# One operand fewer in the step sizes' product, and the residuals' statistics behind the x products

## What is computed

```python
h = h + attn(layernorm(h))            # a selective state-space block, below
h = h + ffn(layernorm(h))             # 32 experts, each token goes to 8
# inside attn, with x = layernorm(h):
zxbcdt = einsum('btd,pd->btp', x, W_in)            # z, x, B, C, dt
dt = softplus(dt_raw + dt_bias)                    # 16 heads
xBC = silu(conv_b + sum(shifted(xBC, k) * conv_w[:, k] for k in range(4)))
# h_t = h_{t-1} * exp(dt_t * A) + dt_t * B_t x_t ;  y_t = h_t C_t + D x_t
y = y * silu(z)
y = y * rsqrt(mean(y * y) + eps) * norm_w
return einsum('bti,di->btd', y, W_out)
```

## Time and profile before

| what | us |
|---|---|
| median of 3 runs | 1726.41 (1725.41 to 1730.03) |
| the profiled execution | 1733.31 |
| its span, first to last instruction | 1731.6 |
| PE busy in the span | 1558.0 (90%) |
| DVE busy | 969.8 (56%) |
| POOL busy | 788.6 (46%) |
| ACT busy | 728.9 (42%) |

### The profile page before, as it was taken

The page is one execution under the profiler, slowest core; times in us unless marked ns, Lnnn a source line. Parts: engine busy times, 40 slices in busy tenths (PEclk is TensorE's granted clock), DMA queues, the critical chain, the costliest instruction groups (busy, mean ns, idle before and its releaser), DMA issues. The chain is left out here.

```text
span 1731.6 us, 31397 instructions
## 1 busy us (share of the span) xinstructions
PE 1558.0 (90%) x9263; PEld 1133.3 (65%) x9264; DVE 969.8 (56%) x2309; ACT 728.9 (42%) x1592; POOL 788.6 (46%) x678
## 2 busy tenths in 40 slices
PE   7999999987699999999999760499999999999997
PEld 7999999984566685775766430265565666565564
DVE  5555554532678989999999454143343434333343
ACT  2525343431856857858658100133333333333332
POOL 4330300011042247777777577455445555454554
PEclk9999999997889999999999575699999999999999
DMA  7210000003444443543532110477677777767665
GB/s 274 80 62 1 13 1 13 1 19 110 144 118 119 130 138 97 156 132 94 157 89 78 33 39 2 158 166 178 162 164 162 161 188 173 180 156 191 157 112 99
DMA packets 97702, 195.19 MB, mean 113 GB/s; under 512 B 38391, under 2 KB 46879, under 8 KB 92880
## 3 DMA queue, kind: packets, MB, share of 16 engines
q0 software_dynamic: 36992, 88.26, 23.4%
q1 hardware_dynamic: 60624, 105.78, 19.9%
HBM read 144.15 MB, written 49.84 MB: 112 GB/s over the span
## 5 line engine op out<-in xcount | busy, mean ns | idle before, releaser
L1902 PE MATMUL moe_ps_gu<-moe_wgu,moe_xt 128*128 x960 | 333.6, 491 | 0.0
L1760 POOL DMA_INDIRECT out_h<-moe_yy,moe_idx_s x121 | 190.8, 1577 | 260.3 <-DVE moe_idx_s L1822 111.0
L1028 POOL DMA_INDIRECT scratch_slots<-lay_toki,lay_slot x192 | 217.9, 1135 | 57.5 <-issue 57.5
L1902 PEld LDWEIGHTS moe_ps_gu<-moe_wgu,moe_xt 128*128 128x128 f32 x960 | 174.4, 192 | 97.0 <-issue 1.8
L1799 ACT ACTIVATE moe_sl<-moe_ps_gu 128x192 f32<-128x192 f32 x120 | 39.6, 330 | 365.0 <-PE moe_ps_gu L1902 365.0
L1299 PE MATMUL lay_ring<-head_wout,lay_yb 128*128 128x512 f32 x384 | 171.2, 600 | 0.0
L1431 DVE SCALAR_TENSOR_TENSOR lay_xa<-lay_ring,head_cw,lay_xa 128x378 f32<-128x378 f32 (+5 forms) x240 | 141.6, 609 | 51.4 <-ACT lay_xa L1086 45.5
L1215 PE MATMUL lay_ring<-lay_xnt,win_sb 128*128 128x128 f32 (+2 forms) x1152 | 163.3, 288 | 1.5 <-ACT lay_xnt L1118 0.7
L1754 POOL DMA_INDIRECT moe_xg<-scratch_xg,moe_idx_g x123 | 131.1, 1066 | 48.0 <-issue 23.9
L1215 PEld LDWEIGHTS lay_ring<-lay_xnt,win_sb 128*128 128x128 f32 (+2 forms) x1152 | 146.5, 195 | 6.9 <-issue 2.1
L247 POOL TENSOR_TENSOR tok_vv<-tok_w 128x512 f32<-128x512 f32 x16 | 16.6, 1038 | 261.4 <-ACT tok_w L449 227.1
(11 more groups left out here) (291 smaller groups left out, 2944.2 us busy)
## 6 DMA issues: line engine op xcount, KB each, us to landing
lay_m<-scratch_cum SPq DMA_DIRECT2D x16, 1536.0 KB
moe_wgu<-in_wgu SPq DMA_DIRECT2D x32, 768.0 KB, 5.7
moe_wd<-in_wd SPq DMA_DIRECT2D x32, 384.0 KB, 7.7
out_h<-lay_hres SPq DMA_DIRECT2D x48, 128.0 KB
scratch_xg<-lay_x SPq DMA_DIRECT2D x48, 128.0 KB
win_sb<-in_win SPq DMA_DIRECT2D x1, 4384.0 KB, 15.9
tok_u_raw<-in_tok_u SPq DMA_DIRECT2D x16, 256.0 KB, 4.4
tok_v_raw<-in_tok_v SPq DMA_DIRECT2D x16, 256.0 KB, 5.1
```

What stands on the lines that cost most here:

```text
L1028: pool.indirect_dma_start(out=a["slots"], out_offset=bass.IndirectOffsetOnAxis(ap=slot[i % 2][:, j, k:k + 1], axis=0), in_=toki[i % 2][:, ...
L1760: pool.indirect_dma_start(out=a["out"], out_offset=bass.IndirectOffsetOnAxis(ap=idx_s[n][:, 0:1], axis=0), in_=yy[n][:], in_offset=None, b ...
L1902: last = mm(ps_gu[b][:], xt[b][:, t], wgu[:, bass.ds(r * KD + t, 1)].rearrange("p o n -> p (o n)"), start=t == 0, stop=t == KD - 1)
```

## The change

Three things. The step sizes' product multiplied the softplus by A (one value per partition) and by a tile of ones that it read in full; now it multiplies by A alone, with one operand of many elements. The three residuals follow each other, and their statistics with the variances' last step form a new function `residual_stats`, which is called behind the six x products. The shift of the routed rows moves behind the convs of B and C.

```diff
-                    own.step(v.scalar_tensor_tensor(dtr[:], td_in[32:48], ea[:], ones[0:NH].unsqueeze(1).to_broadcast([NH, 2, SEQ]),
-                                                    ALU.mult, ALU.mult))
+
+                    own.step(v.tensor_scalar(dtr[:], td_in[32:48], ea[:], None, ALU.mult))
...
-                    dve.wait_ge(res_done, i * 3 + j + 1)
-                    own.step(v.bn_stats(st[:], h[:, j]))
-                    own.step(v.bn_aggr(mv[:, j], st[:]))
-                    if j == 2:
-                        v.tensor_scalar(ve[:], mv[:, :, 1], EPS, None, ALU.add).then_inc(ve2_done, 1)
+
+                def residual_stats(i):
+                    h = hres[i % 2]
+                    for j in range(N_BLK):
+                        dve.wait_ge(res_done, i * 3 + j + 1)
+                        own.step(v.bn_stats(st[:], h[:, j]))
+                        own.step(v.bn_aggr(mv[:, j], st[:]))
+                    v.tensor_scalar(ve[:], mv[:, :, 1], EPS, None, ALU.add).then_inc(ve2_done, 1)
...
                     if pairs(i):
-                        routed_shift(i)
+                        residual_stats(i)
                     if pairs(n + 1):
                         conv(n + 1, 0)
                         conv(n + 1, 1)
+                    if pairs(i):
+                        routed_shift(i)
                     if pairs(n):
                         state_matrix(n, 1)
```

## The result

The changed kernel takes 1766.1 us (median of six runs, 1762.8 to 1772.0) against 1728.5 of the kernel before (six runs, 1725.4 to 1730.9): a ratio of 1.0215, 95% interval 1.0194 to 1.0236. The forecast was 1716. Its profiled execution took 1771.5 us, with a span of 1769.8; before it was 1733.3 and 1731.6.

A forecast was written before the change was run, and what follows sets the result against it. The time from a pair's first residual to its second gating's end was taken to set the pair; 0.2 - 0.7 + 2.4 + 5.0 + 3.4 = 10.3 us off 1726.4 gave 1716.1, range 1705 to 1723.

The forecast's parts named there:

- TensorE's earlier arrival: At the transposes of x: TensorE done 3 us earlier; no new wait at the state products was priced.
- The sum: Whole kernel: 0.2 for the first gating, -0.7 pair 0, 2.4 pair 1, 5.0 pairs 2 to 5, 3.4 pair 6: 10.3 us gained.
- rival (b): TensorE's clock: fewer 1.2 GHz spells, 1708, chance 0.18; or new spells at the silu of z, 1722.9, chance 0.08.
- the part on the moved statistics: VectorE's residuals in a row: x products start 1.8 us after the first residual; conv of B gains 1.4 to 2.7 us.
- rival (a): Step-size product and scans run beside POOL's gating, unheld: 2.3 us for each of three steps, 1709, chance 0.07.
- the sum adds 0.6: POOL's list writes ahead of the first gating: one held 0.6 us longer beside VectorE's step sums.
- the sum has 7.4: Pairs 1 to 5: 2.4 us gained in pair 1 and 5.0 us over pairs 2 to 5.
- the upside that rival (b) named: Low-clock spells behind TensorE's waits vanish, above all in pair 7's state products: 1708, chance 0.18.
- as the sum has it (0.7): Pair 0: all three statistics now stand behind the x products instead of two in VectorE's wait; 0.7 us lost.
- the 3.4 of the sum: Pair 6: state products start 5.6 us after the first residual instead of 9.0, a gain of 3.4 us.
- rival (c): POOL's two gatings stay apart because VectorE reaches the product late: 17.6 us more on the sum, 1733.7, chance 0.05.

The follow-up runs named there:

- e6: Kernel after plus two filling matmuls, their result overwritten unread, between the fourth and fifth state product: 1713.8 us, 0.9880 of before.
- e1: Kernel before with only the new step-size product with one long operand: 1730.0 us, ratio 0.9989.
- e11: Kernel before plus two filling matmuls between the fourth and fifth state product, as a control: 1735.0 us, ratio 1.0019.
- e2: Kernel after with the old step-size product, so only the statistics and the shift moved: 1768.0 us, ratio 1.0198.
- e4: Kernel before, with the fifth state product waiting for both pieces of the state matrix's second half: 1792.4 us, ratio 1.0338.
- e7: Kernel after with the state matrix's second half made in four pieces instead of two: 1761.9 us, ratio 1.0168 against before.
- e8: Kernel after with the first residual's statistics kept between the first and second residual: 1757.5 us, ratio 1.0125 against before.
- e10: Kernel after plus one filling matmul between the fourth and fifth state product: 1722.7 us, ratio 0.9948 against before.
- e9: Kernel after with the state matrix's second half in four pieces and the first statistics kept between residuals: 1739.7 us, ratio 1.0043 against before.

## Why the prediction was wrong

**The step that failed** is TensorE's earlier arrival. The sum has it at nothing, and the sentence "TensorE is now ahead" in rival (b) follows it only to the silu of z. In the part on the moved statistics the transposes are done 3 us earlier, and I followed this lead to the conv of B and to the gatings, but not to TensorE's own next need of VectorE. The rows for it were there to be asked for: the first state product of pair 4 started at T + 10.7 (818.18) and now starts at T + 6.0 (767.32), 4.7 earlier; the second half of the state matrix started at T + 14.7 (822.18) and now starts at T + 12.1 (773.49), 2.5 earlier. The fifth product had no wait and only 0.2 us of slack (824.08, its piece ready at about 822.18 + 1.7), so it had to wait 4.7 - 2.5 - 0.2, and it waits 2.00. Pair 2 gives the same without the short spell that pair 4 had: the first state product 3.3 us earlier (T + 9.3 to T + 6.0), the second half 1.3 (T + 13.4 to T + 12.1). As waiting alone it would have cost next to nothing, since e6 spends these 2 us on matmuls for nobody and its gatings still come as forecast.

**The size** came from the clock. Rival (b) had the right mechanism, a wait moved and a spell behind it, but at the silu of z, at a price of 1.7 us in four pairs and with a chance of 0.08. It was at the fifth state product, 20.5 us long, in six pairs, at a price of 8.3 us. Its cost is read against e6: T of pair 1 is 8.9 us later (610.56 against 601.62), and from there to T of pair 6 the kernel after takes 376.75 us and e6 335.38, 8.3 per pair. That is 50.3 us for six spells, against which the gains stand.

**What came out as written**, in the kernel after itself:
- Three residuals in 2.06 us (1.83 forecast), the first x product at T + 2.0, the conv of B at T + 8.5 (8.4) with no idle time ahead.
- No wait of TensorE at the sixth transposed part.
- One list write held for 4.05 us beside the state matrix, one for 1.26 beside the step sums (0.98 without company), where the sum adds 0.6; the first gating at T + 23.1 (23.7).
- The product at 0.41 us (0.4) where POOL is not gating. Where it is, 3.46 to 3.48 us, as I took from the earlier trace rows against the hope of rival (a). So these engines do not meet only by semaphores. The first of these:

```profile
487.98 3.46 DVE L1417 TENSOR_SCALAR lay_dtr<-lay_td_in,head_ea 16x384 f32<-16x384 f32 x1
```

- Pair 6: the first state product at T + 5.75 (993.06, T = 987.31) against 5.6. The second gating of pair 7 ends 35.4 us behind T (1019.28 + 3.43) where it took 39.7.

**What e6 adds**: with the clock held, T of pair 1 to T of pair 6 takes 335.4 us instead of 347.5, a gain of 12.1 where the sum has 7.4 for these pairs. The excess is time at the low clock that pairs of the kernel before lose (0.95 in pair 1, 0.98 in pair 4) and e6 doesn't: the upside that rival (b) named. The trace of e1, with VectorE's order of before and no spell in these pairs, shows how much: it takes 342.24 us, so 5.2 of the 12.1 are the clock's and 6.9 are left for the sum's 7.4. Pair 0 loses 0.6 us (71.97 to 72.59), as the sum has it (0.7). Behind T of pair 6 e6 gains 10.1 us; of these the kernel after has 3.2, about the 3.4 of the sum, and the other 6.9 come with the filling, which shortens the long spell of the last pair as in e11: the low clock lasts 47.8 us there in the kernel before and 41.0 in the kernel after, but twice 13.7 in e6, and 17.1 and 13.7 in e11. From T of pair 1 to T of pair 6 in e1, then from T of pair 6 to the end in the kernel before and in e6:

```profile
598.78:941.02 342.24, 327.69 (x2274) 227.03 (x2273) 321.98 (x697) 239.17 (x497) 244.31 (x201) 1.00 0.43 120
```

```profile
945.94:1731.60 785.66, 669.16 (x2979) 413.48 (x2977) 316.92 (x1067) 211.35 (x413) 428.07 (x359) 0.91 0.59 137
```

```profile
937.00:1712.60 775.60, 660.73 (x2983) 407.97 (x2981) 317.52 (x1067) 211.54 (x413) 428.40 (x359) 0.92 0.61 139
```

The whole gain of e6, 1.2%, is above the forecast's 0.6, and a part of it is the filling's and not the change's. So the sum was not wrong on VectorE and POOL; it was a sum for a kernel whose TensorE stays at its clock.

The slower rival (c), gatings apart and the second ending at T + 35, describes POOL's rows fairly well (T + 34.1), but for another reason: not VectorE late at the product, but TensorE slow at the state products.

One wait of 1.98 to 2.00 us per pair (1.70 in pair 0), between two groups of matmuls, stands ahead of each spell in the kernel after. The Trainium skill ("TensorE: Matmul & The Clock Gate", "A second HAM failure mode: psum-queue depth-cycling") describes a kernel in which small idle times between groups of matmuls, and not one long wait, make the clock swing between its two levels. The trace agrees in part: here too a short idle time between groups goes with a swing between the two levels, but there is one such wait in some 75 us, where the page has frequent ones. It would have been a reason to look for each new wait and give it a chance of its own.

**What stays open** is where exactly it tips. Waits ahead of the fifth product of 1.62 to 2.00 us brought the spell in all pairs 0 to 5 of the kernel after, e2 and e4, and so did 1.19 us (e7) and 1.04 us (e8) in pairs 1 to 5; pair 0 of these two, with 0.90 and 0.74 us there, had none. In e10, 0.93 or 0.94 us brought it in one of five pairs. In e9 pairs 1 to 5 have the same waits, 0.24 us at the fifth product and 1.21 at the sixth, with the same products around them, and only pair 5 had the spell; pair 0, with nothing but the 1.21, had it too. So neither the length of a wait nor the work around it decides alone, and what else does, no run shows. e10 also leaves open whether its shorter wait or its filling matmul is what spared four pairs that e8 with 1.04 us lost. That the work in a spell is what makes it long is not shown: it is argued from two places only, the projection of B and C in the kernel before (3.4 us) and the state products in the kernel after (20.5 us).

## What to carry to other kernels

When an edit lets an engine come earlier, follow it to the next thing that it waits for, and write down what TensorE does on both sides of that new wait: two waits of 1.08 us ahead of a projection brought 3.4 us at the low clock here, and not in every pair; one of 2.00 us among the state products brought 20.5, in every pair. If TensorE's busy time rises with the same number of instructions, look at the granted clock by stretches before looking for a new bound. A wait that can't be removed may be filled with matmuls whose result nobody reads; here two of them per pair turned a loss of 2.2% into a gain of 1.2%. Before such a gain is put down to the change, add the same filling to the kernel before: here some 7 us of the gain came from the filling in the last pair.

## What was not expected of the hardware

- At 1.2 GHz TensorE stayed busy for 20.5 us without a gap (20.50 of 20.50 us, 122 matmuls) and the granted clock was 0.50 all the while. The first two projections of z still lay in the spell (792.99 to 796.5); at the third the clock was back.
- The long spells of pairs 0 to 5 are nearly equally long whichever edit brings them: 20.5 us in the kernel after and in e2, e4, e7, e8 and e9 (three of them 23.9), 17.1 in the one of e10.
- A product with one long operand in SBUF is held by POOL's gating just as one with two: 3.46 us beside it against 0.41 alone, where the old product has 3.67 and 0.60.
